# One transpose and two wide second-bias products in place of seven transposes and seven tile products, in a patch-embedding, attention and mixture-of-experts kernel

## The chip, the cores and the metric

The kernel runs on one core of one Trainium2 chip. The metric is the time of one execution in device microseconds; lower is better. Five engines work side by side: PE (matrix products; PEld is its loading of the stationary operand), DVE (vector), ACT (activation), POOL (GpSimd) and SP, which here issues most of the DMA transfers.

## The reference, cut to what matters

An input of 64 sequences is cut into 14 patches each, which gives N = 896 tokens of D = 128 numbers, held as NT = 7 tiles of 128 tokens. Tokens go through an attention layer, and then through a block of which this is the part that matters:

```python
logits = rc                                       # 10 experts
vals, idx = top_k(logits, 2)
gates = zeros(N, E).at[rows, idx].set(softmax(vals))
h = elu(x2 @ e_w1 + e_b1)                         # per expert
eo = h @ e_w2 + e_b2[:, None, :]
y = einsum('end,ne->nd', eo, gates)
sh = silu(conv9(x) + sh_b1)
sh = conv1(sh) + sh_b2
z = residual + y + sh                             # then a layer norm
```

The term of the change is the second bias: `gates @ e_b2 + sh_b2`. With a column of ones beside the 10 gates of a token (11 columns), and `sh_b2` as an eleventh row below the ten rows of `e_b2`, it is one product of 11 rows.

## The kernel before, in words

Everything is written by hand, engine by engine, with semaphores between engines; each engine runs its list in order.

The sum z is gathered in two PSUM banks (`Z_BANKS`, 2 and 3), which hold tiles 0 to 3 (called half 0) and tiles 4 to 6 (half 1). Into them go, all by PE: the residual (`residual`, L649), the second bias (`second_bias`, L849), the shared branch's second convolution (`shared_down(hf, c)`, L855, for 4 channel chunks c), the last block of expert outputs (`last_block`, L861), and for half 0 the gathered expert outputs (L893). Every 32-bit product is two matmul instructions in the trace, so a tile of `shared_down` counts two and `x8` is four tiles.

The shared branch's first convolution is done ahead of that, in products L713 over 4 chunks with 4 products (m = 1, 2, 0, 3) each. After product m = 2 of chunk 2 stands `gate_transposes` (the transposes are on L765): seven transposes turn the gates [128 tokens, 7 tiles, 11] tile by tile into rows, into two PSUM banks (4 and 3); ACT copies them to `gatesT` (L1059, two copies), and the products m = 3 of chunk 2 and m = 1 of chunk 3, which use these banks, wait for the copies.

Then the experts. Tokens sorted by expert make NB = 23 blocks of 128 rows. For block j PE transposes the tokens (`block_x`, L728), makes the hidden layer (`block_up`, L741), waits for ACT's exponentials (L1089) and DVE's ELU (L1407, L1409, which make `tb`), and makes the output (`block_down`, L753) into the single bank `Y_BANK`. `block_down(j)` waits for `tb` of block j, and for ACT's copy of block j-1 out of that bank (`block_out`, L1099, which makes `yb`). POOL scatters `yb` to memory (L506) for blocks 0 to 21. When all scatters have landed, SP and ACT each fetch the tokens' rows back, half 1 first (`fetch`, L362). The order on PE ends with

```python
for step in range(2, NB + 3):
    if step < NB: block_x(step)
    if step <= NB: block_up(step - 1)
    else: second_bias(TILES[step - NB - 1])
    if step == 3: shared_down(1, 0)
    if step >= 3: block_down(step - 3)
for hf in (1, 0):
    for c in range(1, HC): shared_down(hf, c)
    ... last_block(hf)
```

so the second bias of half 0 stands between `block_down(20)` and `block_down(21)`, and that of half 1 between `block_down(21)` and `block_down(22)`. Behind that, DVE adds the fetched rows of half 1 (L1427, L1429), takes its statistics and scales (L1435); for half 0 PE adds the fetched rows (L893) and DVE takes the statistics (L1142), scales (L1435) and adds (L1445), and the result is stored.

On SP's queue at the start, the load of the second-bias matrix `b2sh_s` (L388) stands behind the weights and ahead of two fills of memory with zeros (L391, L393).

Of the kernel before, what the change touches and what calls it, by code (L numbers as in the profile page):

```python
# [18 lines left out]
ACT = mybir.ActivationFunctionType  # L19
AX = mybir.AxisListType  # L20

P = 128
# [3 lines left out]
N = B * T  # L26
NT = N // P
D = 128
# [5 lines left out]
E, DHID = 10, 512  # L34
HC = DHID // P
KSH, KRC = 9, 3
HALVES = [(0, 512), (512, N)]
# [15 lines left out]
TILES = [range(0, 4), range(4, NT)]  # L53
# [35 lines left out]
NB = (TOP * N + E * (P - 1)) // P  # L89
# [5 lines left out]
Z_BANKS = (2, 3)  # L95
# [5 lines left out]
M_START = {0: 0, 1: SUM, 2: DIFF, 3: 1}  # L101
M_ORDER = (1, 2, 0, 3)
M_BANK = [{1: 0, 2: 1, 0: 2, 3: 3}, {1: 4, 2: 6, 0: 7, 3: 5}]
G_BANK = (4, 3)
PAIRS = {1: (0, NP), 0: (1, NP), 2: (0, NP - 1)}


# [14 lines left out]
def build(nc, xT, wtok, wqkvo, wrc1, wrc2, wsh1, wsh2, wexp, b2sh, cols, rows, brow, ident, upper, spare_ids, out):  # L122
    with ExitStack() as ctx:
        def sb(name, shape, dt=F32, scope=ctx):
            return scope.enter_context(nc.sbuf_tensor(name, shape, dt))
# [3 lines left out]
        def S(name):  # L129

            if name not in sems:
                sems[name] = ctx.enter_context(nc.semaphore(name))
            return sems[name]
# [21 lines left out]
        upper_s = sb("upper_s", [P, P])  # L155
        upper_b = sb("upper_b", [P, P], BF16)
        ones_b = sb("ones_b", [P, P], BF16)
        b2sh_s = sb("b2sh_s", [E + 1, D])
        zero_s = sb("zero_s", [P, D])
        spare_id = sb("spare_id", [P, NB, XW - D])  # L160
        tsh = raw[:, 0:HC * N].rearrange("p (c n) -> p c n", c=HC)
# [8 lines left out]
        xnT = sb("xnT", [P, N])  # L170
        cT = sb("cT", [P, N])

        gatesT = cT[0:E + 1]
        on, h2, zt = x1, h, xnT[:].rearrange("p (i d) -> p i d", d=D)
        spare = xT_s[:].rearrange("p a j b -> p (a j b)")
        x3e = spare[:, 0:TOP * NT * XW].rearrange("p (k i d) -> p k i d", k=TOP, d=XW)
# [338 lines left out]
        def _(pe):  # L515
# [202 lines left out]
            def block_x(j):  # L718

                for k, (a, _) in enumerate(LOADS):  # L720
                    if j == a:
                        pe.wait_ge(S(f"ld_xb{k}"), 16)
                if j < 2:
                    pe.wait_ge(S("c1_done"), HC)
                else:
                    pe.wait_ge(S("xTb_done"), j - 1)
                col = P if j == 1 else 0
                nc.tensor.transpose(ps[X_BANK][:, col:col + P], xb[:, j, 0:D], ident_s[:]).then_inc(S("xTb_mm"), 1)  # L728
# [25 lines left out]
                             start=(c == 0), stop=(c == HC - 1))  # L754
                ins.then_inc(S("down_mm"), 1)

            def gate_transposes():

                pe.wait_ge(S("gates_done"), 1)
                pe.wait_ge(S("c1_done"), 2)  # L760
                pe.wait_ge(S("y1_done"), 1)
                for hf in (1, 0):
                    for i in TILES[hf]:
                        col = (i - TILES[hf][0]) * P
                        ins = nc.tensor.transpose(ps[G_BANK[hf]][0:E + 1, col:col + P], gates[:, i, :], ident_s[:])  # L765
                    ins.then_inc(S("gT_mm"), 1)

            pe.wait_ge(S("ld_rc"), 32)
            pe.wait_ge(S("rc_split"), 1)
# [64 lines left out]
            for c in range(2, HC):  # L834
                for m, done in zip(M_ORDER, ("c1_done", "uv_done", "y0_done", "y1_done")):
                    pe.wait_ge(S(done), c - 1)
                    if c == 2 and m == 3:
                        pe.wait_ge(S("gT_done"), 1)
                    if c == 3 and m == 1:
                        pe.wait_ge(S("gT_done"), 2)  # L840
                    for part in range(3):
                        product(c, m, part, part == 2)
                    if c == 2 and m == 2:
                        gate_transposes()

            def second_bias(tiles):

                for i in tiles:
                    mm(z_ps[i], gatesT[:, i * P:(i + 1) * P], b2sh_s[:], start=False, stop=False)  # L849

            def shared_down(hf, c):

                pe.wait_ge(S("tsh_done"), c + 1)
                for i in TILES[hf]:
                    ins = mm(z_ps[i], tsh[:, c, i * P:(i + 1) * P], wsh2_s[:, c, :], start=False,  # L855
                             stop=False)
# [10 lines left out]
            pe.wait_ge(S("ld_b2"), 16)  # L867
            residual(Z_BANKS[0], x3, TILES[0])
            shared_down(0, 0)
            block_x(0)  # L870
            block_x(1)
            residual(Z_BANKS[1], x3, TILES[1])
            block_up(0)
            for step in range(2, NB + 3):
                if step < NB:
                    block_x(step)
                if step <= NB:
                    block_up(step - 1)
                else:
                    second_bias(TILES[step - NB - 1])  # L880
                if step == 3:
                    shared_down(1, 0)
                if step >= 3:
                    block_down(step - 3)
            for hf in (1, 0):
                for c in range(1, HC):
                    shared_down(hf, c)
                pe.wait_ge(S("hot_done"), 1)
                pe.wait_ge(S("yb_done"), NB)
                last_block(hf)  # L890
# [14 lines left out]
        def _(act):  # L905
# [146 lines left out]
                    act.wait_ge(S("tsh_done"), c - 1)  # L1052
                A(ex[c % 2], rr[c % 2], ACT.Tanh).then_inc(S("a2_done"), 1)

            def gates_in_rows(k):

                act.wait_ge(S("gT_mm"), 2 - k)
                lo, hi = HALVES[k]
                A(gatesT[:, lo:hi], ps[G_BANK[k]][0:E + 1, 0:hi - lo], ACT.Copy).then_inc(S("gT_done"), 1)  # L1059

            A(gel_s[:, 1:2], cols_s[:, C_ZERO:C_ZERO + 1], ACT.Exp).then_inc(S("exp_table"), 1)
            first_sum(0)
# [5 lines left out]
            first_sum(1)  # L1068
            tanh(0)
            first_sum(2)  # L1070
            for hf in (1, 0):
                gates_in_rows(hf)
            tanh(1)
            first_sum(3)
            tanh(2)
# [396 lines left out]
    return (np.array([k * N + i for k in range(TOP) for i in range(NT)])[None] + NT * np.arange(P)[:, None]).astype(np.float32)  # L1472


def spare_numbers():

    ids = TOP * N + np.arange(NB)[None] * P + np.arange(P)[:, None]
    return np.stack([ids, np.zeros_like(ids)], axis=2).astype(np.float32)
# [51 lines left out]
```

## Time and profile before

| | us |
|---|---|
| three runs: lowest, median, highest | 161.65, 162.09, 162.22 |
| profiled execution: span from first to last instruction | 161.2 |
| PE busy | 151.8 |
| DVE busy | 129.0 |
| POOL busy | 87.0 |
| ACT busy | 78.2 |

The profile is one execution of its own; its span leaves out what lies ahead of the first and behind the last instruction, and no other time is reported for it. Busy time of PE is modelled from instruction sizes, so overlapping matmuls can look longer than the step from one to the next; the chain of waits gives the steps. "PEclk" is the granted TensorE clock as a share of full speed. A row of the chain is: start, length, engine, tile and line, count of instructions.

### The profile page before, as it was taken

The page shows a single profiled execution, that of the slowest core. Times are in us where ns is not written, and L with a number is a line of the kernel's source. Part 1 is how long each engine was busy: PE and PEld are TensorE (multiplying, and loading weights), DVE is VectorE, ACT ScalarE, POOL GpSimd, SP SyncE. Part 2 cuts the span into 40 slices and gives each one's busy share as a digit, 9 for nine tenths or more (in the row PEclk, how much of TensorE's full clock was granted, in tenths as well). Part 3 has the DMA queues.
Part 4 walks back from the last instruction along what each step waited for, and adds up shares of the span by engine and source line. Part 5 has one row for each costly group of instructions (what it writes and reads, how often), then busy time and mean ns, then how long its engine had stood idle before and what let it go on. Part 6 is the DMA issues. An engine that isn't in the chain of part 4 may idle for free.

```text
span 161.2 us, 3074 instructions
## 1 busy us (share of the span) xinstructions
PE 151.8 (94%) x1015; PEld 135.7 (84%) x1015; DVE 129.0 (80%) x347; ACT 78.2 (49%) x195; POOL 87.0 (54%) x77
## 2 busy tenths in 40 slices
PE   7799899999999999999999999999999999999950
PEld 2598689899975649889999988999999999999830
DVE  0169999979998999879977666999999999890762
ACT  2323947201035778951044326677777777811040
POOL 1073799999999683003777710164555554450230
PEclk9999999999999999999999999999999999987999
DMA  4999999965950000000397139999998992005204
GB/s 150 285 417 403 266 210 253 209 83 98 195 98 2 0 0 6 0 0 0 76 333 281 52 88 311 400 396 336 314 295 323 321 310 83 34 32 156 92 0 114
DMA packets 19553, 28.30 MB, mean 176 GB/s; under 512 B 4838, under 2 KB 14193, under 8 KB 19538
## 3 DMA queue, kind: packets, MB, share of 16 engines
q1 hardware_dynamic: 16918, 21.42, 43.1%
q0 software_dynamic: 1696, 5.52, 14.2%
q10 hardware_dynamic: 924, 1.17, 2.4%
q8 instruction: 8, 0.13, 0.3%
q14 instruction: 7, 0.06, 0.1%
HBM read 19.67 MB, written 5.28 MB: 155 GB/s over the span
## 4 chain that ended last, share of the span: by engine, by line
PE 80%; DVE 10%; DMA 4%; ACT 1%; issue 1%; POOL 1%; SPq 0%; DVEq 0%
PE psum L713 16%; PE psum L753 14%; PE psum L624 13%; PE psum L741 12%; PE psum L555 5%; PE psum L855 4%; DMA xT_s<-xT 4%; PE psum L532 3%; PE psum L549 2%; PE psum L649 2%; DVE stats L1142 2%; PE psum L728 2%; DVE raw L1287 1%; PE psum L668 1%; PE psum L849 1%; PE psum L800 1%
## 5 line engine op out<-in xcount | busy, mean ns | idle before, releaser
L506 POOL DMA_INDIRECT ys_rows<-yb,xid x22 | 21.5, 978 | 25.8 <-ACT yb L1099 18.2
L1089 ACT ACTIVATE wu<-psum,wring 128x128 f32<-128x128 f32 x92 | 26.0, 371 | 9.5 <-PE psum L741 8.7
L1409 DVE SCALAR_TENSOR_TENSOR tb<-psum,wring,wu 128x128 f32<-128x128 f32 x92 | 25.9, 344 | 0.8
L753 PE MATMUL psum<-wring,tb 128*128 128x128 f32 x184 | 25.5, 283 | 0.1
L741 PE MATMUL psum<-xTb,wring 128*128 128x128 f32 x184 | 24.3, 275 | 0.0
L753 PEld LDWEIGHTS psum<-wring,tb 128*128 128x128 f32 x184 | 22.9, 196 | 0.6 <-DVE tb L1409 0.3
L496 POOL DMA_INDIRECT xs_rows<-xT_s,slot x14 | 14.0, 998 | 17.2 <-DVE slot L1341 13.2
L741 PEld LDWEIGHTS psum<-xTb,wring 128*128 128x128 f32 x184 | 22.4, 192 | 0.5 <-issue 0.5
L624 PE MATMUL psum<-prod,ident_s 128*128 128x196 f32 (+1 forms) x120 | 21.6, 341 | 0.0
L624 PEld LDWEIGHTS psum<-prod,ident_s 128*128 128x128 f32 x120 | 21.1, 190 | 0.0
L357 POOL TENSOR_TENSOR prod<-es,vt 128x3136 f32<-128x3136 f32 x3 | 19.3, 6519 | 0.0
L1099 ACT ACTIVATE yb<-psum,cols_s,xb 128x128 f32<-128x128 f32 x23 | 10.9, 473 | 4.7 <-PE psum L753 4.7
L713 PE MATMUL psum<-dsf_l,wu_h 128*128 128x384 f32 (+1 forms) x48 | 11.4, 349 | 0.2 <-DVE dsf_l L1293 0.2
L713 PE MATMUL psum<-dsf_h,wu_h 128*128 128x384 f32 (+1 forms) x48 | 11.5, 350 | 0.0
L713 PE MATMUL psum<-dsf_h,wu_l 128*128 128x384 f32 (+1 forms) x48 | 11.4, 349 | 0.0
L1407 DVE TENSOR_SCALAR wu<-wu 128x512 f32<-128x512 f32 (+1 forms) x24 | 10.1, 422 | 1.1 <-ACT wu L1089 1.1
L345 DVE TENSOR_TENSOR prod<-psum,kt 128x3136 f32<-128x3136 f32 x3 | 10.2, 3418 | 0.0
L436 POOL TENSOR_TENSOR rstd<-veps,mhalf 128x2 f32<-128x2 f32 (+1 forms) x9 | 6.9, 774 | 5.2 <-DVE veps L1151 3.4
L713 PEld LDWEIGHTS psum<-dsf_l,wu_h 128*128 128x128 f32 x48 | 8.7, 188 | 0.8 <-DVE dsf_l L1293 0.5
L713 PEld LDWEIGHTS psum<-dsf_h,wu_l 128*128 128x128 f32 x48 | 8.7, 188 | 0.3
L713 PEld LDWEIGHTS psum<-dsf_h,wu_h 128*128 128x128 f32 x48 | 8.7, 188 | 0.3
L555 PE MATMUL psum<-wqkvo_s,xnT 128*128 128x128 f32 x56 | 8.0, 286 | 0.6 <-ACT xnT L927 0.6
(181 smaller groups left out, 277.4 us busy)
## 6 DMA issues: line engine op xcount, KB each, us to landing
wring<-wexp SPq DMA_DIRECT2D x23, 514.0 KB, 5.3
wu<-raw POOLq DMA_DIRECT2D x2, 1536.0 KB, 11.7
raw<-wsh SPq DMA_DIRECT2D x2, 768.0 KB, 9.2
xs_rows<-zero_s SPq DMA_DIRECT2D x1, 1472.0 KB, 15.0
ys_rows<-zero_s SPq DMA_DIRECT2D x1, 896.0 KB, 16.9
xT_s<-xT SPq DMA_DIRECT2D x2, 384.0 KB, 5.8
wu<-wsh SPq DMA_DIRECT2D x1, 768.0 KB, 7.6
xb<-xs_rows SPq DMA_DIRECT2D x1, 585.0 KB, 6.2
```

Of the source, the lines that this page charges most:

```text
L345: return engine.tensor_tensor(o_ap, q_ap, k_ap, ALU.mult)
L357: return engine.tensor_tensor(o_ap, e_ap, v_ap, ALU.mult)
L496: pool.indirect_dma_start(xs_dram, bass.IndirectOffsetOnAxis(ap=slot[:, n:n + 1], axis=0), x3e[:, n // NT, n % NT, :], None)\
L506: pool.indirect_dma_start(ys_dram, bass.IndirectOffsetOnAxis(ap=xid[:, j:j + 1], axis=0), yb[:, j % NY, :], None)\
L555: ins = mm(ps[bank][:, a:a + D], xnT[:, i * P:(i + 1) * P], wqkvo_s[:, n, :], start=False, stop=(i == tiles[-1]))
L624: ins = mm(o_ap, ident_s[:], src[:, k * w:(k + 1) * w], start=(k == 0), stop=(k == n - 1))
L713: ins = mm(ps[M_BANK[c % 2][m]][:, qa * B:qb * B], w[:, g, c * P:(c + 1) * P], x[:, a:a + 2 * (qb - qa) - 1:2, :], start=(part == 0 and g ...
L741: ins = mm(ps[U_BANKS[j % NU]][:, c * P:(c + 1) * P], wring[:, j % NR, c * P:(c + 1) * P], xTb[:, j % 2, :], start=True, stop=True)
L753: ins = mm(ps[Y_BANK][:, 0:D], tb[:, j % NTT, c, :], wring[:, j % NR, W2 + c * P:W2 + (c + 1) * P], start=(c == 0), stop=(c == HC - 1))
L1089: ins = A(eb[:, j % NEB, c, :], ps[U_BANKS[j % NU]][:, c * P:(c + 1) * P], ACT.Exp, bias=wring[:, j % NR, B1 + c:B1 + c + 1])
L1099: A(yb[:, j % NY, :], ps[Y_BANK][:, 0:D], ACT.Identity, bias=cols_s[:, C_ZERO:C_ZERO + 1], scale=xb[:, j, X_GATE:X_GATE + 1]).then_inc(S(" ...
L1409: ins = V.scalar_tensor_tensor(tb[:, j % NTT, c, :], ps[U_BANKS[j % NU]][:, c * P:(c + 1) * P], wring[:, j % NR, B1 + c:B1 + c + 1], eb[:, ...
```

## The change

The 7 x 11 gate columns are transposed by one transpose, into 77 rows x 128 tokens in one bank (4), and copied by ACT once. The second-bias matrix becomes 77 rows x 896 columns, which holds for tile i the 11 rows in its own 128 columns and zeros elsewhere, so that one product with the 77 rows as stationary operand gives all tiles of a half: one of 512 columns and one of 384. The product of half 0 moves to behind `shared_down(0, 0)`, ahead of the blocks; that of half 1 to behind the block loop; `shared_down(0, 1)` moves from the end to the place between `block_down(21)` and `block_down(22)`; between `block_down(20)` and `block_down(21)` nothing is left. The load of `b2sh_s` grows accordingly.

```diff
-G_BANK = (4, 3)
+GATE_BANK = 4
...
-        b2sh_s = sb("b2sh_s", [E + 1, D])
+        b2sh_s = sb("b2sh_s", [NT * (E + 1), N])
...
-        gatesT = cT[0:E + 1]
+        gatesT = cT[0:NT * (E + 1), 0:P]
...
-            def gate_transposes():
+            def gate_transpose():
 
                 pe.wait_ge(S("gates_done"), 1)
                 pe.wait_ge(S("c1_done"), 2)
-                pe.wait_ge(S("y1_done"), 1)
-                for hf in (1, 0):
-                    for i in TILES[hf]:
-                        col = (i - TILES[hf][0]) * P
-                        ins = nc.tensor.transpose(ps[G_BANK[hf]][0:E + 1, col:col + P], gates[:, i, :], ident_s[:])
-                    ins.then_inc(S("gT_mm"), 1)
+                nc.tensor.transpose(ps[GATE_BANK][0:NT * (E + 1), 0:P], gates[:].rearrange("p i e -> p (i e)"), ident_s[:])\
+                    .then_inc(S("gT_mm"), 1)
...
-                    if c == 2 and m == 3:
+                    if c == 3 and m == 1:
                         pe.wait_ge(S("gT_done"), 1)
-                    if c == 3 and m == 1:
-                        pe.wait_ge(S("gT_done"), 2)
                     for part in range(3):
                         product(c, m, part, part == 2)
                     if c == 2 and m == 2:
-                        gate_transposes()
-
-            def second_bias(tiles):
-
-                for i in tiles:
-                    mm(z_ps[i], gatesT[:, i * P:(i + 1) * P], b2sh_s[:], start=False, stop=False)
+                        gate_transpose()
+
+            def second_bias(hf):
+
+                lo, hi = HALVES[hf]
+                mm(ps[Z_BANKS[hf]][:, 0:hi - lo], gatesT, b2sh_s[:, lo:hi], start=False, stop=False)
...
             residual(Z_BANKS[0], x3, TILES[0])
             shared_down(0, 0)
+            second_bias(0)
             block_x(0)
             block_x(1)
             residual(Z_BANKS[1], x3, TILES[1])
...
                 if step <= NB:
                     block_up(step - 1)
-                else:
-                    second_bias(TILES[step - NB - 1])
+                if step == NB + 2:
+                    shared_down(0, 1)
                 if step == 3:
                     shared_down(1, 0)
                 if step >= 3:
                     block_down(step - 3)
+            second_bias(1)
             for hf in (1, 0):
-                for c in range(1, HC):
+                for c in range(2 - hf, HC):
                     shared_down(hf, c)
...
-            def gates_in_rows(k):
-
-                act.wait_ge(S("gT_mm"), 2 - k)
-                lo, hi = HALVES[k]
-                A(gatesT[:, lo:hi], ps[G_BANK[k]][0:E + 1, 0:hi - lo], ACT.Copy).then_inc(S("gT_done"), 1)
+            def gates_in_rows():
+
+                act.wait_ge(S("gT_mm"), 1)
+                A(gatesT, ps[GATE_BANK][0:NT * (E + 1), 0:P], ACT.Copy).then_inc(S("gT_done"), 1)
...
+def by_tile_diagonal(rows):
+
+    out = np.zeros((NT, len(rows), NT, D), np.float32)
+    for i in range(NT):
+        out[i, :, i] = rows
+    return out.reshape(NT * len(rows), N)
...
-        "b2sh": _np.concatenate([f("e_b2"), f("sh_b2")[None]]),
+        "b2sh": by_tile_diagonal(_np.concatenate([f("e_b2"), f("sh_b2")[None]])),
```

## Rows read from the trace of the kernel before

**Rows 1.** Part 1 of the page: busy time and share of each engine.
```profile
PE 151.8 (94%) x1015; PEld 135.7 (84%) x1015; DVE 129.0 (80%) x347; ACT 78.2 (49%) x195; POOL 87.0 (54%) x77
```
**Rows 2.** Chain of waits, 137 to 155 us: start, length, engine, line, instructions.
```profile
137.71 0.90 PE psum L753 x8
...
140.51 1.08 PE psum L849 x8
141.59 1.09 PE psum L753 x8
142.68 0.86 PE psum L849 x6
143.54 1.83 PE psum L753 x8
145.37 2.89 PE psum L855 x18
...
152.51 1.73 PE psum L893 x4
...
154.26 0.90 DVE stats L1142 x4
```
**Rows 3.** Stretches of 1 us: length, busy (count) of PE to POOL, PEclk, DMA.
```profile
142.00:143.00 1.00, 1.00 (x10) 0.88 (x9) 0.90 (x6) 0.28 (x1) 0.26 (x1) 1.00 0.16 66
143.00:144.00 1.00, 1.00 (x8) 0.88 (x8) 1.00 (x2) 0.17 (x1) 0.55 (x1) 0.84 0.01 0
144.00:145.00 1.00, 1.00 (x7) 1.00 (x7) 0.95 (x1) 0.00 (x0) 0.79 (x1) 0.50 0.00 0
...
147.00:148.00 1.00, 1.00 (x11) 1.00 (x10) 0.00 (x0) 0.00 (x0) 0.00 (x0) 0.95 0.76 114
```
**Rows 4.** Chain of waits, 83 to 97 us.
```profile
83.93 0.76 PE psum L765 x7
...
94.65 0.86 PE psum L649 x2
95.51 0.89 PE psum L855 x8
```
**Rows 5.** Timeline, PE's weight loads around 96 us, with the idle time before.
```profile
96.44 0.20 PEld L728 LDWEIGHTS psum<-ident_s,xb 128*128 128x128 f32 x2 [0.23 <-DMA xb<-xs_rows]
```
**Rows 6.** Chain of waits, 22 to 30 us: products of 33 rows (L549), full-height L555.
```profile
22.29 0.31 PE psum L549
...
28.67 0.43 PE psum L549
29.10 1.09 PE psum L555 x8
```
**Rows 7.** Timeline of all engines, 137 to 155 us: start, length, instruction, idle before.
```profile
139.45 1.13 DVE L1409 SCALAR_TENSOR_TENSOR tb<-psum,wring,wu 128x128 f32<-128x128 f32 x4
...
140.55 0.48 ACT L1099 ACTIVATE yb<-psum,cols_s,xb 128x128 f32<-128x128 f32 x1
...
143.45 1.34 POOL L506 DMA_INDIRECT ys_rows<-yb,xid  x1 [1.19 <-ACT yb L1099]
...
146.12 0.86 ACTq L362 DMA_DIRECT2D wring<-ys_rows  x2
...
149.70 0.56 DVE L1427 TENSOR_TENSOR xnT<-psum,wring 128x384 f32<-128x384 f32 x1 [4.75 <-DMA wring<-ys_rows]
...
152.03 0.87 DVE L1435 SCALAR_TENSOR_TENSOR x<-xnT,mv,rows_s 128x128 f32<-128x128 f32 x3
```
**Rows 8.** Line L362, the four fetches: time from issue to landing.
```profile
DMA to landing us min/median/max: 3.5/4.1/4.6
```
**Rows 9.** Timeline of SP's queue, start of the kernel: loads of the bias matrix.
```profile
9.69 0.43 SPq L388 DMA_DIRECT2D b2sh_s<-b2sh  x1
```
**Rows 10.** A stretch of 2 us, 36 to 38 us: the last three columns are PEclk, DMA share, GB/s.
```profile
36.00:38.00 2.00, 2.00 (x13) 2.00 (x12) 1.97 (x4) 0.78 (x2) 2.00 (x3) 1.00 0.00 0
```
**Rows 11.** Timeline, PE's weight loads of the first `block_down`.
```profile
101.32 0.97 PEld L753 LDWEIGHTS psum<-wring,tb 128*128 128x128 f32 x8 [0.31 <-DVE tb L1409]
```

More of the change, by code:

```diff
@@ L1070, in _ @@
             first_sum(2)
-            for hf in (1, 0):
-                gates_in_rows(hf)
+            gates_in_rows()
             tanh(1)
```

## The prediction, made before the changed kernel was run

> **What bounds the kernel now.** I read the busy shares first: PE is busy for 151.8 of 161.2 us [rows 1], so work taken off PE is worth looking for, but only where PE sets the pace. The chain of waits tells where. Around the gates (84 us) and again from the block loop to 154 us it lies on PE without a gap [rows 2, 4]. At 154.26 it passes to DVE, which waited for PE's last sum of half 0; from there it is DVE, then the store. So both places that the change touches are on the path, and the question is what else is nearly as late there.
>
> Next I read the granted clock in the tail, stretch by stretch. It is 1.00 (2.4 GHz) up to 143 us, 0.84 in the stretch from 143, 0.50 (1.2 GHz) from 144 to 147, and 0.95 in the stretch from 147 [rows 3]; at 145 and 146 it is 0.50 too. That is 0.32 + 3 x 1.00 + 0.10 = 3.42 us at half speed, and 1.71 us of PE's work lost. The chain shows the loss: 18 instructions of the shared branch take 2.89 us, 0.161 each, where at full clock 8 take 0.89, 0.111 each [rows 2, 4]. It is the only fall before PE's work ends. What PE did just before is the second bias: 14 products with 11 of the 128 rows, in 1.08 + 0.86 us [rows 2], with PE counted busy all the time [rows 3]. So I take the fall to be brought on by these low products and the waits beside them, not by an idle PE.
>
> They cost more than their length in another way. Eight full-height instructions take 0.90 us, and eight of 11 rows take 1.08; the eight full-height ones behind them take 1.09 [rows 2]. Each border between the two heights costs some 0.19 us. There are four such borders in the tail.
>
> **The gates.** Seven transposes take 0.76 us of the chain [rows 4], 0.109 each; one is left: 0.76 - 0.11 = 0.65 us less, all on the path. Two waits there go as well, and the one that stays (product m = 1 of chunk 3 on the copy in bank 4) has a whole product, nine matmuls of chunk 2, between it and the transpose. The copy on ACT is one of 128 columns where there were two of 384 and 512, and ACT is idle about half the time [rows 1]: nothing.
>
> **The second bias of half 0.** It now stands ahead of the blocks: one wide product of 512 columns. Nearest is the residual, 512 columns at full height, 0.86 us [rows 4]. PE reaches the first block's transpose at 95.51 + 0.89 = 96.40 now, and there its load waits for the tokens' landing until 96.44 [rows 4, 5]; that landing hangs on POOL's scatters, not on PE. After: 96.40 - 0.65 + 0.86 = 96.61, 0.17 us later than 96.44. So almost the whole gain of the transposes goes into this product, with 0.04 lost to the landing. From here PE is fed without a gap, so the block loop runs **0.17 us late**.
>
> What a border costs at 77 rows the trace does not show. The low end is nothing, as between full-height products. The high end is what 33 rows show: 512 columns take 0.43 us and 256 take 0.31, so 256 columns cost 0.12 and 0.19 is left over for the border; and the eight full-height ones behind take 1.09 in place of 0.89 or 0.90 [rows 2, 4, 6]. I take nothing, since a product that fills more than half the array is by its use of it nearer to the full one, and keep 2 x 0.2 = 0.4 us for the range.
>
> The Trainium skill's page TensorEngine Tiling (Key Properties) says that changing the tiling mode drains the engine, and its list of modes has row tiles of 32 and 64 rows. The rows above agree for 11 and 33 rows; 77 fit no such tile, so by the page the border costs nothing, the lateness 0.17; by the 33-row rows alone it would be 0.57.
>
> **The tail.** Times are on the old clock, with the 0.17 put in at the end. The second bias no longer covers the wait between `block_down(20)` and `block_down(21)`. The latter needs DVE's `tb` of block 21 (139.45 + 1.13 = 140.58) and ACT's copy of block 20, 140.55 + 0.48 = 141.03 [rows 7]. ACT comes to that copy only after its exponentials, so it does not move. PE stands idle from about 140.5 to 141.07 and `block_down(21)` starts there; its first load came at 141.52 before (0.07 ahead of the chain's 141.59), so it starts and ends **0.45 us earlier**, at 142.23.
>
> Then PE has work without a wait: by the chain's steps the next group starts at about 142.07; `shared_down(0, 1)` 0.89 to 142.96 (by then DVE's last `tb`, due two groups of 0.90 behind the one above at 142.4, is there), `block_down(22)` 0.90 to 143.86, the wide product of 384 columns 0.86 x 384/512 = 0.65 to 144.51, 18 of the shared branch at 0.111, 2.00, to 146.5, the last block's six 0.67 to 147.2, 16 more 1.78 to 149.0 (there were 24), the last block's eight 0.89 to **149.86** (all at 0.111 each). It was 152.51, so PE comes to L893 2.6 us earlier: the lost clock 1.7, and borders, narrow products and their order for the rest, with the wait paid.
>
> What is late next is the fetch. SP and ACT issue it at 146.12, when the last scatter, issued by POOL at 143.45 behind ACT's copy of block 21, has landed [rows 7]. The second issue on each queue is some 0.4 later and lands after up to 4.6 us: 146.12 + 0.4 + 4.6 = 151.1 [rows 7, 8]. With block 21 0.45 earlier it lands at 150.65, which is later than PE's 149.86. So L893 starts at 150.65 and not at 149.86; from there it is a weight load that nothing hides, 0.20 [rows 5], then the 1.75 from 152.51 to 154.26 [rows 2]: 152.6. DVE's own work on half 1 is in the same place: from 149.70 to 152.90 now [rows 7], waiting for the fetch alone, so 149.25 to 152.45 after. DVE starts on half 0 at 152.6 in place of 154.26: 1.66 us earlier. Behind it nothing changes.
>
> Sum: 1.66 - 0.17 = **1.49 us less**. The profiled span is 161.2, the median of the runs 162.09, 0.9 above it; with the same surround 162.09 - 1.49 = **160.6 us**. Bounds: with borders at their full price 161.0; with DVE's own 152.45 the limit, 160.45.
>
> **The bias matrix's load.** 77 x 896 x 4 bytes are 276 KB for 5.5 KB, at 9.69 us on SP's queue behind all weights [rows 9], so it delays only the fills and POOL's weight sums that share the engines. The transfers end with a free stretch, share 0.00 from 36 to 38 us [rows 10]. The four fetches, 896 KB that share the engines, land within some 5 us of the first issue [rows 8], so 276 KB are an estimated 1.5 us of transfer, less than that free stretch: nothing. Without that gap, POOL's second weight sum, and then ACT's copies, would come later by up to that much.
>
> **Rivals.** (a) *The fall of the clock stays.* If it comes from the tail's waits (PE still stands 0.56 us at 140.5) and not from the low products, PE loses 1.71 us after 143.7 again: L893 at 149.86 + 1.71 = 151.57, DVE at 153.5, 0.76 - 0.17 = 0.6 less: **161.5**. Against it: the same kind of wait, 0.31 us at 101 [rows 11], brought none. The page TensorE: Matmul & The Clock Gate of the Trainium skill (Why this matters for your kernels) has the clock fall after PE-idle gaps between bursts; the busy PE of rows 3 speaks against that as the cause, and by it the low products would be innocent and this rival would hold. Chance 0.13.
>
> (b) *The fetch does not come earlier.* POOL's last scatter takes 1.34 us [rows 7] while DVE writes the final block's selection beside it; if POOL is held until DVE is through, it ends no sooner. Then L893 starts at 151.1, DVE at 153.05: 1.2 - 0.17 = 1.04 less, **161.05**. For it: DVE's work beside it stays where it is. Against it: nothing in the trace shows POOL held. Chance 0.17.
>
> (c) *Slower.* The lost cover at 140.5 and the later wait for the fetch let the clock fall sooner and stay down for two such stretches, 6.8 us: PE loses 3.4, L893 at 153.3, DVE at 155.2, 0.95 + 0.17 more: **163.2**. It turns to slower when PE loses over 2.3 us, 4.6 us at half clock. Against it: PE's products from 142 to 150 are all full height but one of 77 rows. Chance 0.04.
>
> **How the numbers follow.** My forecast has 0.66, (a) 0.13, (b) 0.17, (c) 0.04. Half a per cent, 0.8 us, is about what a measurement of this kernel can tell from no change; under 161.3 counts as faster. That holds the forecast nearly whole and (b), 0.81; (a) and what the forecast loses by unforeseen waits count as the same, 0.14; (c) and a mistake in the order of waits, 0.05. The range goes from 160.0 (forecast, with the fetch's landing faster) to 161.5, which takes in (b), the borders' upper price and (a).
>
> **What would show it.** In the new profile: one transpose of 77 columns at 84 us; the first block's transpose released by PE and not by the tokens' landing; PE idle for some 0.5 us ahead of `block_down(21)`; a granted clock of 1.00 through 143 to 148; the wide products at 0.86 and 0.65 us; L893 released by the fetch; DVE without the 1.4 us wait at L1142. A clock of 0.50 in the tail, or an unmoved fetch, says which rival holds; a block loop over 0.5 us late says that the border was mis-sized.

## The result, and the profile after

The changed kernel took 162.81 us (median of 15 runs, 161.80 to 163.60) where the kernel before took 162.02 in the same comparison (15 runs, 161.19 to 163.33): ratio 1.0054, 95% interval 1.0034 to 1.0075. Forecast were 160.6 us and a range of 160.0 to 161.5. It became slower by half a per cent, and in none of these runs was it faster than 161.8. A repetition in another comparison (label `f1_after_again`, below) found 0.2 per cent, which is not to be told from none. Medians are of all executions; ratios leave out those more than 1.5% above the fastest of the same kernel.

The profiled execution took 162.81 us, its span 161.0. The difference, 1.8 us, is what lies around the span; it was 1.74 to 1.92 in all runs of this study. I had taken 0.9, from a span and a median that did not belong to the same execution. With 1.8 around it, the profiled execution of before took some 163.0 us: it was not one of the three that were timed at 161.65 to 162.22, but a longer one. The kernel before was therefore run and profiled again (label `e1_before_again`, 161.68 us, span 159.9). Below, its rows stand beside those of after. In the changed kernel the second bias is L843, the shared branch L849, the last block L855, the sum of the fetched rows L889 and DVE's statistics L1136.

Busy shares of after, against [rows 1]: PE has 2.0 us less to do, and the kernel is longer.

```profile
PE 149.8 (93%) x999; PEld 132.6 (82%) x999; DVE 128.6 (80%) x347; ACT 77.6 (48%) x194; POOL 87.3 (54%) x77
```

**Ahead of the blocks.** Chain of waits of after, 83 to 98 us, against [rows 4]:

```profile
91.14 0.96 POOL xs_rows L496
...
92.41 2.90 DMA xs_rows<-xT_s,slot
...
95.33 2.11 DMA xb<-xs_rows
...
97.48 0.44 PE psum L728 x2
```

The same stretch of the chain, kernel before run again:

```profile
92.05 2.27 DMA xs_rows<-xT_s,slot
...
94.33 2.24 DMA xb<-xs_rows
...
96.61 0.44 PE psum L728 x2
```

In both, the chain lies on POOL's fourteen scatters, the landing of the last one, and the load of the blocks' tokens that SP issues then. In [rows 4] it lay on PE, because PE and the tokens came within 0.23 us of each other [rows 5]. Between the two rows of landing, one number has changed: the last scatter takes 2.90 us to land in place of 2.27. PE's own work is as short as forecast, as its timeline (first row: products of 77 rows; second: the first block's weights, with the wait) shows:

```profile
96.00 1.02 PE L843 MATMUL psum<-b2sh_s,cT 77*128 77x512 f32 x2
...
97.48 0.20 PEld L728 LDWEIGHTS psum<-ident_s,xb 128*128 128x128 f32 x2 [1.28 <-DMA xb<-xs_rows]
```

PE's weight loads wait 1.28 us for the tokens, where they waited 0.23 [rows 5].

**The tail.** The granted clock of after, in stretches of 1 us as in [rows 3]:

```profile
143.00:144.00 1.00, 1.00 (x11) 1.00 (x10) 0.90 (x6) 0.46 (x1) 0.34 (x1) 1.00 0.10 41
144.00:145.00 1.00, 1.00 (x11) 1.00 (x10) 1.00 (x2) 0.00 (x0) 0.85 (x1) 1.00 0.15 41
```

and of the kernel before, run again:

```profile
143.00:144.00 1.00, 1.00 (x9) 0.88 (x9) 0.98 (x1) 0.33 (x1) 0.39 (x1) 1.00 0.17 66
144.00:145.00 1.00, 1.00 (x12) 1.00 (x11) 1.00 (x2) 0.18 (x1) 0.95 (x1) 1.00 0.07 16
```

There is no fall in the tail after (its clock is 0.95 in the two microseconds from 156 and 0.50 from 158, behind the sum of half 0), and there is none before either, with the same fourteen products of 11 rows. The chain of the tail, after, against [rows 2]:

```profile
144.15 3.20 DMA ys_rows<-yb,xid
...
147.80 4.17 DMA wring<-ys_rows
...
152.01 2.00 PE psum L889 x4
...
154.04 0.90 DVE stats L1136 x4
```

and before, run again:

```profile
144.79 2.01 PE psum L855 x18
...
151.04 1.97 PE psum L893 x4
...
153.03 0.90 DVE stats L1142 x4
```

DVE's statistics stood at 153.03 and not at 154.26 [rows 2] in an undisturbed tail. Where [rows 2] had the 18 products of the shared branch at 2.89 us, they take 2.01. What ends the wait at the sum of the fetched rows is the fetch, in both kernels; timeline of PE's weight loads, after:

```profile
152.01 0.30 PEld L889 LDWEIGHTS psum<-wring,ident_s 128*128 128x128 f32 x2 [1.03 <-DMA wring<-ys_rows]
```

and before, run again:

```profile
151.00 0.30 PEld L893 LDWEIGHTS psum<-wring,ident_s 128*128 128x128 f32 x2 [0.16 <-DMA wring<-ys_rows]
```

So PE had next to nothing to give back to the tail, 0.16 us: what it saves there turns into a wait of 1.03 us. From the first block to DVE's statistics it is 56.56 us after (97.48 to 154.04) and 56.42 before (96.61 to 153.03).

### The profile page after: what moved, and what is told of

Its sections match the earlier page's. It is cut to its first block, busy times and chain, and to the rows that moved or that the text cites. A ratio compares the mean times of both kernels' runs of the same rounds, so it can differ in the third digit from the quotient of the medians.

```text
span 161.0 us, 3040 instructions
## 1 busy us (share of the span) xinstructions
PE 149.8 (93%) x999; PEld 132.6 (82%) x999; DVE 128.6 (80%) x347; ACT 77.6 (48%) x194; POOL 87.3 (54%) x77
## 4 chain that ended last, share of the span: by engine, by line
PE 59%; DMA 11%; DVE 11%; POOL 9%; issue 5%; ACT 2%; SPq 0%; DVEq 0%; POOLq 0%
PE psum L624 13%; PE psum L753 12%; PE psum L741 12%; POOL xs_rows L496 8%; PE psum L555 5%; PE psum L532 4%; DMA xT_s<-xT 4%; PE psum L713 3%; DMA wring<-ys_rows 3%; PE psum L549 2%; DMA ys_rows<-yb,xid 2%; DMA xs_rows<-xT_s,slot 2%; DVE stats L1136 2%; PE psum L728 2%; DVE raw L1281 1%
## 5 line engine op out<-in xcount | busy, mean ns | idle before, releaser
L753 PE MATMUL psum<-wring,tb 128*128 128x128 f32 x184 | 24.7, 277 | 0.8 <-ACT yb L1093 0.7
L753 PEld LDWEIGHTS psum<-wring,tb 128*128 128x128 f32 x184 | 22.3, 191 | 1.2 <-DVE tb L1403 1.1
L1391 DVE COPY xTb<-psum 128x128 f32<-128x128 f32 x21 | 6.1, 290 | 3.5 <-PE psum L728 2.2
```

The costliest lines, as they stand in the source:

```text
L753: ins = mm(ps[Y_BANK][:, 0:D], tb[:, j % NTT, c, :], wring[:, j % NR, W2 + c * P:W2 + (c + 1) * P], start=(c == 0), stop=(c == HC - 1))
```

## The experiments

What had to be told apart: whether the fall of the clock belonged to the kernel or to one execution; which of the parts (big load, order, wide products, one transpose) makes it slower; and why the last scatter lands later. Letters in the quotes stand for theories, and a letter can mean another theory in another quote; the text beside them says in words what was found. Each kernel is named by its label, and each ratio is to the kernel before on the same chip.

**The kernel before, unchanged.** No edit.

> The kernel before, unchanged, to see its spans and clocks run by run. Theory A (the profiled execution of before was not a usual one: the fall of the clock in the tail comes in few executions, so what the change takes away there was hardly paid): spans of about 160.2 us at the median time of 162.0, mean clock 0.99 and more in most runs, and a profile with a granted clock of 1.00 in the tail up to 150 us, DVE's last statistics some 1.2 us sooner after the start of the block loop than in the first profile. Theory B (the fall is usual, and the change loses its gain elsewhere): mean clock about 0.988 in most runs and a fall in the tail again.

Ratio 0.9984 (0.9953 to 1.0015), 161.87 us in 12 runs. Its profile has the full clock in the tail (above). Of its 12 runs one had a mean granted clock of 0.978, and that one took 163.03 us, the longest; all others had 0.990 or more. A fall of 3.42 us to half speed, as in [rows 3], takes the mean of 161.2 us down to 0.989 by itself (that execution had 0.988), so none of the eleven can have had it whole. It is thus something that happens in some executions of the same program. What starts it was not found.

**The big load alone.**

```diff
-        b2sh_s = sb("b2sh_s", [E + 1, D])
+        b2sh_s = sb("b2sh_s", [NT * (E + 1), N])
...
-                    mm(z_ps[i], gatesT[:, i * P:(i + 1) * P], b2sh_s[:], start=False, stop=False)
+                    mm(z_ps[i], gatesT[:, i * P:(i + 1) * P], b2sh_s[0:E + 1, 0:D], start=False, stop=False)
```

> Kernel before with the 276 KB bias matrix loaded in place of 5.5 KB; everything else as before (the products read its first 11 rows and 128 columns). Theory L (the load delays the fills, the weight sums or the start): slower than before by 0.5 to 0.9 us, with the first attention context, POOL's first scatter or the first block later by as much against the first products. Rival (the load is hidden, as predicted): within 0.2 us of before.

Ratio 1.0018 (0.998 to 1.0057). The transfers end later, in the free stretch; 34 to 38 us, with the big load:

```profile
34.00:36.00 2.00, 2.00 (x14) 2.00 (x13) 1.15 (x5) 0.37 (x1) 2.00 (x1) 1.00 0.73 46
36.00:38.00 2.00, 2.00 (x12) 2.00 (x11) 1.97 (x4) 0.78 (x2) 1.92 (x3) 1.00 0.08 1
```

and without:

```profile
34.00:36.00 2.00, 2.00 (x13) 2.00 (x12) 1.18 (x4) 0.37 (x1) 2.00 (x1) 1.00 0.33 58
```

The share rises from 0.33 to 0.73 in the first stretch and from 0.00 [rows 10] to 0.08 in the second: 2 x 0.40 + 2 x 0.08 = 0.96 us of the free stretch are used, of an estimated 1.5, and no engine's busy time moves by more than 0.08 us. By the ratio alone the load could still cost half a per cent; the first block is not late (table below), and the wide products with PE held back (below) carry the same load without loss. The load is not the cause.

**The new order alone**, with the narrow products: `second_bias(TILES[0])` behind `shared_down(0, 0)`, `shared_down(0, 1)` at step NB + 2, `second_bias(TILES[1])` behind the loop.

```diff
             shared_down(0, 0)
+            second_bias(TILES[0])
...
-                else:
-                    second_bias(TILES[step - NB - 1])
+                if step == NB + 2:
+                    shared_down(0, 1)
```

> Kernel before with its seven transposes, narrow products and small load, but in the new order: the products of half 0 behind shared_down(0, 0), of half 1 behind the block loop, shared_down(0, 1) between block_down 21 and 22. Theory O (the new order costs the time): 0.6 to 1.2 us slower than before, with the block loop starting later by up to the length of the products, 1.3 us. Rival W: within 0.3 us of before.

Ratio 1.001 (0.9977 to 1.0043). The first block starts at 97.84 here, without a wait for its tokens: PE is the later one. The order by itself makes no difference that this comparison can tell.

**The wide products and the one transpose, in the old order.** The changed kernel with the order taken back:

```diff
-            second_bias(0)
...
-                if step == NB + 2:
-                    shared_down(0, 1)
+                if step > NB:
+                    second_bias(step - NB - 1)
```

> The changed kernel with its one transpose, wide products and large load, but in the old order: wide product of half 0 between block_down 20 and 21, of half 1 between 21 and 22, and all of shared_down at the end. Theory O (the new order costs the time: the product ahead of the blocks and the lost cover): faster than the changed kernel by 0.6 to 1.0 us, at or below before. Rival W (the wide products or the load cost it): as slow as the changed kernel, 0.6 to 0.9 us over before.

Ratio 1.0039 (1.0006 to 1.0073). So it is slower too, without the new order. Its profiled execution took 164.99 us against a median of 163.08, and only its head is used here. PE's wait for the tokens is the longest of all. Its row in the timeline:

```profile
97.61 0.20 PEld L728 LDWEIGHTS psum<-ident_s,xb 128*128 128x128 f32 x2 [2.04 <-DMA xb<-xs_rows]
```

and the stretches of 1 us behind it, with the granted clock third from the end:

```profile
98.00:99.00 1.00, 1.00 (x7) 0.54 (x5) 0.00 (x0) 0.38 (x1) 0.00 (x0) 0.97 1.01 277
99.00:100.00 1.00, 1.00 (x7) 1.00 (x6) 0.00 (x0) 0.00 (x0) 0.00 (x0) 0.50 1.11 322
```

In this execution the clock fell to its lower level (1.2 GHz) a little over a microsecond after PE's weight loads had stood for 2.04 us (its products 1.84); its mean clock was 0.981 here, and 0.989 or more in the kernel's other executions.

**The same, with PE kept as late as before.** The one transpose is made seven times, which gives PE back the 0.65 us:

```diff
-                nc.tensor.transpose(ps[GATE_BANK][0:NT * (E + 1), 0:P], gates[:].rearrange("p i e -> p (i e)"), ident_s[:])\
-                    .then_inc(S("gT_mm"), 1)
+                for _ in range(7):
+                    ins = nc.tensor.transpose(ps[GATE_BANK][0:NT * (E + 1), 0:P], gates[:].rearrange("p i e -> p (i e)"), ident_s[:])
+                ins.then_inc(S("gT_mm"), 1)
```

> The wide products in the old order, with the one transpose of 77 columns made seven times over, so that PE comes to the end of the convolution when it did before. Theory C (PE's code load: the 0.65 us that PE is early puts an 8 KB load of its code on the DMA engine that still has a piece of POOL's last scatter to write, which lands 0.6 to 1.1 us later and holds the first block): the code load is behind the scatter again, from issue to landing of the last scatter takes 2.3 us as in the kernel before, and the time comes back from 0.4 per cent over to within 0.2 per cent of before. Rival W (the wide products or the large matrix cost it): as slow as the wide products in the old order, 0.4 per cent or more over before.

Ratio 0.997 (0.9935 to 1.0005), and 0.9999 in the repetition below: more work on PE, and less time than the kernel without it (1.0039), each against the kernel before of its own comparison. The chain ahead of the blocks is back where it was:

```profile
92.04 2.32 DMA xs_rows<-xT_s,slot
...
94.38 2.22 DMA xb<-xs_rows
...
96.64 0.44 PE psum L728 x2
```

**The reverse: the kernel before, with PE early.** Six of the seven transposes are left out, ACT copies one tile per half, and the product that waited for the first copy no longer does. The second bias of five tiles is then made from other numbers; no product is left out.

```diff
-                for hf in (1, 0):
-                    for i in TILES[hf]:
-                        col = (i - TILES[hf][0]) * P
-                        ins = nc.tensor.transpose(ps[G_BANK[hf]][0:E + 1, col:col + P], gates[:, i, :], ident_s[:])
-                    ins.then_inc(S("gT_mm"), 1)
+                nc.tensor.transpose(ps[G_BANK[0]][0:E + 1, 0:P], gates[:, 0, :], ident_s[:]).then_inc(S("gT_mm"), 2)
```

> Kernel before with six of the seven transposes of the gates left out, and ACT copying one tile per half (so five tiles' second bias is made from other numbers); the order, the narrow products and the small matrix are those of before. PE is 0.65 us early ahead of the blocks, as in the changed kernel. Theory C: though work is left out, the code load meets the last scatter, which lands 0.6 us or more later, and the kernel is 0.3 to 0.8 us slower than before. Rival (an early PE only waits longer): within 0.2 us of before.

Ratio 1.0055 (1.0019 to 1.0092), 162.94 us: work taken away, nothing added, and it is slower by as much as the changed kernel. The SP row of its timeline is at 95.18, 2.96 us behind the last scatter's issue at 92.22:

```profile
92.22 0.96 POOL L496 DMA_INDIRECT xs_rows<-xT_s,slot  x1 [0.31 <-issue]
95.18 2.07 SPq L409 DMA_DIRECT2D xb<-xs_rows  x4
```

**What delays the scatter.** The DMA view by short stretches names it. After, 93.9 to 94.2 us (queue, kind: packets, MB, share of 16 engines):

```profile
q0 software_dynamic: 22, 0.06, 63.0%
q14 instruction: 1, 0.01, 9.7%
```

and before, 93.4 to 93.9 us, the stretch in which all of the scatter's packets lie:

```profile
q0 software_dynamic: 32, 0.07, 40.9%
```

and 94.2 to 94.6 us:

```profile
q14 instruction: 1, 0.01, 9.8%
```

q0 carries POOL's scatters: 16 pieces of 4160 bytes and 16 completion marks. q14 brings 8 KB of program code. It moves with PE: in twelve of the fourteen traces it comes 0.26 to 0.31 us ahead of the residual's first product (L649), wherever that is. Before, it comes behind the scatter; after, among its packets. No record says whose code it is, but PE's own program does not place it: when it comes, PE has begun between 552 and 585 of its weight loads and waits, and DVE 190 of its instructions in all fourteen traces. In the same twelve it comes 1.09 to 1.14 us behind the start of the 190th, DVE's L1359 (L1353 after), which waits for one of PE's products; the next one on DVE waits for another. So the code is that of an engine that follows PE there. DVE fits; ACT and POOL, with 87 or 88 and 66 instructions begun, are not ruled out. The packets' records of all traces, in us from the issue of the last scatter:

```
                        code load    last piece  last mark  SP issues  first block
                        from  to     starts      done       xb load    starts
before                  2.27  2.89   1.70        1.89       2.28       4.47
e1 before again         2.23  2.94   1.70        1.89       2.28       4.56
e2 big load             2.25  2.87   1.70        1.89       2.28       4.45
e4 narrow, new order    2.50  2.81   1.70        1.89       2.28       5.46 (PE)
e5 wide, hold           2.25  2.82   1.70        1.89       2.34       4.60
g1 wide, hold, again    2.24  2.79   1.70        1.89       2.28       4.50
e6 before, DVE held     2.25  2.81   1.70        1.89       2.34       4.59
f2 after, hold          2.24  2.99   1.70        1.89       2.41       4.72
after                   1.55  2.01   2.01        2.25       2.92       5.07
f1 after again          1.56  2.25   2.25        2.55       3.22       5.48
f3 after, pad           1.55  2.24   2.24        2.50       3.16       5.43
e7 after, DVE held      1.57  2.03   2.03        2.27       2.94       5.26
e8 few transposes       1.58  2.08   2.08        2.28       2.96       5.13
e3 wide, old order      2.01  2.32   2.32        2.71       3.38       5.63
```

In the six traces whose PE comes early, the scatter's last piece starts in the very moment in which the code load ends; in the other eight the load comes when the pieces are through. In five of the six the load begins at the same place, 1.55 to 1.58, and by itself takes 0.46 to 0.69 us: the last piece follows its end, from 2.01 to 2.25, also between two executions of the same kernel (after and f1). So it is the load that the piece waits for, and not something else in PE's being early. The scatter counts as landed with its last piece, so one piece of 4 KB behind one load of 8 KB holds SP's issue by 0.6 to 1.1 us, and with it the whole block loop. Of that, 0.36 to 0.82 us is gone when the last mark is done; some 0.28 more lie between that mark and SP's issue, and the records do not say why. In e3 the recorded load begins only after the other pieces; why its last piece had not gone before is not seen. (At 106 us such loads come in pairs of 8 KB; a first one without a record would explain it, which is not shown.)

The Trainium skill's page Runtime: NRT & Kernel Launch (Instruction fetch mechanics) says that each engine's sequencer fetches its next code by a DMA queue of its own, at a cost that is mostly hidden. The traces show two queues that bring code, q8 and q14; the pad below shows that q8 goes by PE's program. The cost of the load on q14 is hidden from PE, which shows no stop there, but not from the scatter.

**The changed kernel with PE held back, and with its code moved**, beside the changed kernel itself. The first has the seven transposes of the diff above. The second cuts the warm-up products at the start:

```diff
-            keep_going(FILL[0], XT_BANK[0])
+            for _ in range(4 * FILL[0]):
+                mm(ps[XT_BANK[0]][:, 0:P], ones_b[:], ones_b[:], start=True, stop=True)
```

> The changed kernel once more, beside the two below on one chip. Both theories: 0.3 to 0.8% slower than before; the last token scatter (L496) is issued 2.9 us or more ahead of SP's issue of the blocks' first load, PE's load of code (8 KB) lies in the middle of that scatter's packets, and PE reaches the first block some 0.8 to 1.3 us before the tokens land (first block at 97.3 to 97.6 us).

> The changed kernel with its one transpose made seven times, so PE reaches the stretch ahead of the blocks 0.65 us later. Theory A (an early PE loads its code into the last scatter's packets): the load falls behind the scatter, the step from last scatter to SP's issue shrinks from 2.9 to 2.3 us, the first block starts at 97.2 (now PE's own time, with the 0.86 us of the wide product ahead of it), 0.2 to 0.4 us sooner than in the changed kernel although PE does 0.65 us more work; the median is 0.1 to 0.5 us below the changed kernel's. Rival B (work put back costs its length): 0.3 to 0.65 us above the changed kernel's.

> The changed kernel with its eleven first warm-up products of 512 columns cut into 44 of 128, which takes the same 4.5 us and puts 33 products more into PE's program ahead of everything else, so that PE's loads of code come at other places of its list. Theory A: the 8 KB load that came at 94.0 us comes some us sooner or later, away from the last scatter; the step from last scatter to SP's issue is 2.3 us, the first block starts at 96.6 to 96.9 us, 0.6 to 1.0 us sooner, and the median is 0.4 to 1.0 us below the changed kernel's, with the same work on PE. Rival B (it is PE's being early that delays the scatter, by something else than the load): step 2.9 us and median as in the changed kernel. If the load stays beside the residual at 94 us, the run tells nothing apart.

Measured: the changed kernel 1.0023 (0.9991 to 1.0055), 162.94 us; held back 1.0021 (0.9989 to 1.0053), 162.48 us; padded 1.0025 (0.9987 to 1.0062), 162.96 us. The hold moves the load behind the scatter, as expected (table), and SP's issue follows the scatter sooner (2.41 us behind its start, 3.22 in the changed kernel beside it):

```profile
91.61 0.95 POOL L496 DMA_INDIRECT xs_rows<-xT_s,slot  x1 [0.30 <-issue]
94.02 2.07 SPq L409 DMA_DIRECT2D xb<-xs_rows  x4
```

The first block starts 4.72 us behind the scatter's issue in place of 5.48. The time does not grow by the 0.65 us put back, which speaks against the rival, but the two ratios cannot be told apart: the medians differ by 0.46 us, as expected, the means by 0.24, give or take 0.25.

The pad missed its aim, and tells something else. The load on q14 stayed at the same place of the work, in spite of 33 products more ahead of it: when it comes PE has begun 585 weight loads and waits, in the changed kernel 552, and DVE 190 instructions in both. The 16 KB loads on q8, the other queue with code, did move: all eight come 1.2 to 6.3 us sooner than in the changed kernel beside it (the fourth, for one, at 77.55 us in place of 83.89), while the last scatter is issued 0.47 us sooner. So q8 brings PE's code, and the load on q14, which delays the scatter, is another engine's, brought forward by PE's early products. Since the pad could not move it, no run moved this load without moving PE.

**The scatter in the tail.** The second thing to explain is why a last expert block that comes 0.37 us sooner after the loop's start (`block_down(21)` stands in the chain at 142.25 - 97.48 = 44.77 us, and before, run again, at 141.75 - 96.61 = 45.14) brings nothing. POOL's scatter and DVE's sum in the timeline, after:

```profile
144.15 1.71 POOL L506 DMA_INDIRECT ys_rows<-yb,xid  x1 [0.81 <-ACT yb L1093]
...
144.95 1.08 DVE L1417 TENSOR_TENSOR h<-h,rows_s 128x896 f32<-128x896 f32 x1
```

and before, run again:

```profile
143.61 1.34 POOL L506 DMA_INDIRECT ys_rows<-yb,xid  x1 [1.19 <-ACT yb L1099]
...
144.03 1.09 DVE L1423 TENSOR_TENSOR h<-h,rows_s 128x896 f32<-128x896 f32 x1
```

The scatter takes 1.71 in place of 1.34 us; the blocks' other scatters take 0.96. It ends 0.17 us ahead of the end of DVE's sum in both (145.86 and 146.03, 144.95 and 145.12). Two kernels hold DVE's selection (with the three small operations ahead of it) and the sum back until this scatter has landed:

```diff
+            dve.wait_ge(S(f"ys_out{(NB - 2) % NY}"), 16 * ((NB - 2) // NY + 1))
             link(V.tensor_scalar(tok[:, 0:1], last_id, float(N), float(N), ALU.is_ge, ALU.mult))
```

> Kernel before, with DVE's selection of the last block's tokens and its addition to h2 held until POOL's last scatter has landed. Theory D (POOL is held by these two operations of DVE while it makes the scatter's descriptors, and the fetch behind it sets the end): the scatter takes 0.96 us in place of 1.34, the fetch is issued 0.4 us sooner, the time falls by 0.2 to 0.4 us. Rival (PE's sums are as late as the fetch): no more than 0.1 us.

> The changed kernel with the same hold of DVE's two operations. Theory D: the scatter takes 0.96 us in place of 1.71, the fetch is issued 0.75 us sooner after the block loop's start, and PE, which had been waiting for it, uses all of it: 0.6 to 0.8 us less than the changed kernel, about the time of before. Rival (the fetch lands by the speed of its transfers): within 0.2 us of the changed kernel.

Ratios 1.0107 (1.0072 to 1.0141) and 1.0063 (1.0027 to 1.01). Half of what was expected came: the scatter takes 0.96 us in both, so DVE is what stretches it. The page SBUF — State Buffer of the Trainium skill (SBUF: two separate sides) says that a DMA issued by GpSimd waits for its descriptors while DVE holds the ports that the two share. These rows agree that DVE delays it, but not for the whole of its work: the scatter ends 0.17 us ahead of DVE's sum. The other half did not come. Kernel before with DVE held, chain (from the scatter's issue):

```profile
143.49 3.15 DMA ys_rows<-yb,xid
...
146.67 0.16 DVE tok L1419
...
147.25 1.10 DVE ex L1422
...
148.40 0.94 PE psum L861 x6
```

The scatter (0.96 us in its timeline row, from 143.49) still lands at 146.65, and the selection that DVE now writes late holds PE's last block to 148.40. Here too a code load is in the way: the DMA view of 144.3 to 145.5 us has one of 16 KB, on another queue,

```profile
q8 instruction: 1, 0.02, 6.5%
```

and the packets' records show it from 144.33 to 145.57, fifteen pieces from 145.03 on, and the sixteenth at 145.59. With DVE not held (before, run again) the load runs from 144.42 to 145.57 and the first piece starts at 145.53; the last mark is at 146.08 in both. DVE hides the load's cost, and the load hides DVE's. A hold of the sum alone, with the selection left in place, was not tried.

**The best version once more.** The wide products in the old order with the hold:

> The two wide products in the old order, with the one transpose made seven times, once more and in more rounds, since its first comparison (0.997, 0.9935 to 1.0005) left open whether it beats the kernel before. Theory A (code load behind the last scatter, block loop where it was; wide products in the tail worth little, since DVE and PE wait for the fetch there): first block at 96.4 to 96.7 us, ratio 0.995 to 1.000. Rival (the wide products shorten the tail by their 1 us): ratio 0.993 or less.

Ratio 0.9999 (0.9964 to 1.0035), first block at 96.75, 162.14 us against 162.2. With the first comparison (0.997), it is not to be told from the kernel before. The wide products themselves do what they should: in e5's tail the one of 512 columns takes a step of 0.86 us (140.55 to 141.41 in PE's timeline) where eight narrow matmuls took 1.08; PE then waits 0.88 us for the fetch:

```profile
151.21 0.30 PEld L888 LDWEIGHTS psum<-wring,ident_s 128*128 128x128 f32 x2 [0.88 <-DMA wring<-ys_rows]
```

## Why the prediction was wrong

**The clock** was the step that failed by most: "So I take the fall to be brought on by these low products and the waits beside them". One execution showed it, and the kernel before with the same products runs without it. Counted from the loop's start, DVE's statistics stood at 154.26 - 96.44 = 57.82 us in that execution and at 56.42 in the undisturbed one: 1.40 of the forecast 1.66 us in the tail were there only in it. After, they stand at 56.56, where the forecast had 152.6 - 96.44 = 56.16: what the tail would be was forecast within 0.40 us, what it was before was not. That 0.40 is in part luck: the fetch was issued 0.71 us later after the loop's start than forecast (49.94 against 145.67 - 96.44 = 49.23), and landed within 4.55 us (147.42 to 151.97) where 5.0 had been allowed. The surround would have warned: with 1.8 in place of 0.9 the profiled execution comes to 163.0, beyond all three runs. The median to start from already held an undisturbed tail.

**The gates**: the size was right. In the changed kernel's timeline the one transpose's weights are loaded at 84.00 and the next product's at 84.18, a step of 0.18 us where seven took 0.76. The prediction let the wide product use up that gain, and PE's side came out: its last product ahead of the blocks ends at 96.00 + 0.86 = 96.86, 4.45 us behind the last scatter's issue (92.41), where the forecast had 96.61 - 91.97 = 4.64. "All on the path" was wrong. The tokens already came last, by 0.04 us [rows 4, 5]; on their branch, POOL's scatters, nothing was made shorter, so an earlier PE could win nothing there.

**"That landing hangs on POOL's scatters, not on PE"**, and so "the block loop runs 0.17 us late": this is the step that made it slower. The issue of the scatters does not hang on PE, their landing does, through a load of another engine's code that PE's early arrival brings forward. The loop starts 0.87 us late against the kernel before run again: 0.64 from the landing, 0.36 because the whole execution ran that much later already (scatter at 92.41 against 92.05, not seen as a rule), less 0.13 at the load's landing. 0.64 of 162 us is 0.4%, against 0.4 to 0.55% in the ratios of after, e3 and e8, and 0.2% in the changed kernel's repetition.

**The border of 77 rows**: taken as nothing, and nothing it is (0.86 us for 512 columns, as for the full-height residual, and 0.64 for 384, from 145.01 to 145.65 in PE's timeline of after). The reason given, that it fills more than half the array, was not tested. The sign set for a mis-sized border, a block loop over 0.5 us late, came for another reason. **The load**: nothing, as forecast. **`block_down(21)`** came 0.37 us sooner after the loop's start, 0.45 forecast.

**The fetch**: rival (b), to which I gave 0.17, holds in its mechanism. The scatter is stretched by DVE from 1.34 to 1.71 us, so all 0.37 are given back, and what came next, the fetch, is issued hardly sooner after the loop's start than before: 147.42 - 97.48 = 49.94 against 146.72 - 96.61 = 50.11. The forecast's own starting point, 146.12, also belonged to the execution with the fallen clock: 49.68 us after its loop's start. There the 16 KB load on q8 comes at 146.95, behind the scatter, and in the undisturbed one at 144.42, just ahead of its pieces. The rival's time (161.05) was still too low, because it was worked out on the clock's fall as well. Rivals (a) and (c) had the clock fall after; it did not, in the profiled run. No rival had a slower kernel without the clock.

## What to carry to other kernels

Before a stall of the profile is put on the kernel's account, compare the profiled execution's own time with the timed runs; if it is the longer one, the stall may be that execution's. Where two branches meet within some tenths of a microsecond, shortening one of them wins those tenths at most, and an engine that comes early brings others early, with their loads of program code: look in the DMA view for what lands in that moment. An engine that waits for a transfer can be given more work at no cost; in e5 that took back what coming early had cost.

## What the runs showed of the hardware that was not expected

- A code load of 8 KB (0.31 to 0.75 us) holds one piece of a small scatter until it ends, and the scatter's completion reaches SP 0.6 to 1.1 us later; one of 16 KB took 1.24 us and did the same to one of the 16 pieces of another scatter.
- 33 products more on PE bring the 16 KB loads on q8 1.2 to 6.3 us forward and leave the 8 KB loads on q14 at the same place of the work: the first go by PE's program, the second do not.
- DVE's operations stretch POOL's issue of a scatter from 0.96 to 1.34 and 1.71 us.
- The clock can fall to half after PE's weight loads have stood for 2.04 us (one execution of e3), and in single executions also with PE counted busy [rows 3]; most executions of the same program don't show the second.
